# Global attention with exchanged halves by copies, merged sums and a new prologue; biases of the sparse projections added by VectorE

## The reference, cut to what matters

```
Q, K, V = x @ Wq.T + bq, x @ Wk.T + bk, x @ Wv.T + bv      # 16 heads of 8
q_scores = 0.5*norm(Q) + 0.3*entropy(softmax(Q)) + 0.2*var(Q, ddof=1)
```

```
def _rotate_half(x):
    x1, x2 = jnp.split(x, 2, axis=-1)
    return jnp.concatenate((-x2, x1), axis=-1)
q = q * cos + _rotate_half(q) * sin
k = k * cos + _rotate_half(k) * sin
attn = softmax(q @ k.T * SCALE)
return (attn @ v) @ Wo + bo
```

## Time and profile before

| | us |
|---|---|
| median of 3 runs | 3885.16 (3882.11 to 3892.41) |
| the profiled execution's own time | 3877.67 |
| its span | 3875.9 |
| PE busy | 3460.4 (89%) |
| DVE busy | 2522.3 (65%) |
| ACT busy | 1832.9 (47%) |
| POOL busy | 1613.7 (42%) |

### The profile page before, as it was taken

How to read it: one execution, slowest core, us unless ns; L and a number is a source line. 1 busy time by engine, 2 the same in 40 slices (tenths; PEclk the granted TensorE clock), 3 DMA queues, 4 the chain that set the end, 5 groups by cost and what they waited for, 6 DMA issues and landing times. The chain is left out here.

```text
span 3875.9 us, 61610 instructions
## 1 busy us (share of the span) xinstructions
PE 3460.4 (89%) x23550; PEld 2161.1 (56%) x23550; DVE 2522.3 (65%) x4730; ACT 1832.9 (47%) x3269; POOL 1613.7 (42%) x1100
## 2 busy tenths in 40 slices
PE   6999999999857647999669999999999999978997
PEld 4777787878756435777523333333333333336776
DVE  4565656565655456777567777677677766757776
ACT  2344444434323124999423334333433333339997
POOL 1212121111104123666225556556655666656664
PEclk9999999999988557999879999999999999989999
DMA  2000000000010001000100000000000000010000
GB/s 94 1 1 1 1 1 1 1 1 1 1 45 9 6 0 44 2 2 2 38 0 1 1 1 1 1 1 1 1 1 1 1 1 1 1 44 2 2 2 12
DMA packets 21486, 31.46 MB, mean 8 GB/s; under 512 B 8418, under 2 KB 17932, under 8 KB 19724
## 3 DMA queue, kind: packets, MB, share of 16 engines
q1 hardware_dynamic: 21196, 27.52, 2.3%
HBM read 26.46 MB, written 1.05 MB: 7 GB/s over the span
## 5 line engine op out<-in xcount | busy, mean ns | idle before, releaser
L3027 POOL TENSOR_TENSOR global_acc_pool<-global_acc_pool,global_probs 128x1024 f32<-128x1024 f32 x320 | 776.7, 2427 | 470.6 <-ACT global_probs L2980 452.6
L2980 ACT ACTIVATE global_probs<-global_ps 128x1024 f32<-128x1024 f32 x512 | 524.7, 1025 | 883.2 <-PE global_ps L2853 856.9
L3075 DVE TENSOR_REDUCE global_part<-global_ps 128x2 f32<-128x1024 f32 x512 | 624.7, 1220 | 428.9 <-PE global_ps L2835 428.7
L2853 PE MATMUL global_ps<-global_q,global_k 64*128 64x512 f32 x2048 | 522.4, 588 | 0.0
L2864 PE MATMUL global_ps<-global_probs,global_v 128*64 128x512 f32 x2048 | 495.7, 605 | 0.0
L2835 PE MATMUL global_ps<-global_khh,global_qhh 64*128 64x512 f32 x1024 | 324.9, 631 | 35.9 <-DVE global_part L3075 33.9
L994 DVE COPY_PREDICATED delta_Y<-delta_tri,delta_ps 128x512 f32<-128x512 uint32 x192 | 140.4, 731 | 290.9 <-PE delta_ps L533 290.9
L900 POOL TENSOR_TENSOR delta_gm<-C_tile,delta_g 128x1024 f32<-128x1024 f32 x16 | 30.4, 1897 | 718.9 <-PE delta_ps L453 685.3
L2851 PE MATMUL global_ps<-global_mrow,global_first 64*128 64x512 f32 x1024 | 323.6, 629 | 0.0
L2864 PEld LDWEIGHTS global_ps<-global_probs,global_v 128*64 128x64 f32 x2048 | 124.3, 136 | 282.6 <-issue 161.4
L2835 PEld LDWEIGHTS global_ps<-global_khh,global_qhh 64*128 64x128 f32 x1024 | 97.9, 188 | 323.0 <-DVE global_part L3075 259.3
(11 more groups left out here) (587 smaller groups left out, 6862.3 us busy)
## 6 DMA issues: line engine op xcount, KB each, us to landing
delta_cw<-in_conv_taps SPq DMA_DIRECT2D x4, 1024.0 KB, 11.5
local_tab<-in_rot_tables SPq DMA_DIRECT2D x2, 2048.0 KB, 12.3
local_tab<-in_rot_tables SPq DMA_DIRECT2D x2, 1536.0 KB, 7.9
localw_wqkv<-in_L_ffn_wqkv SPq DMA_DIRECT2D x2, 768.0 KB
delta_wqkvz<-in_L_attn_a_W_qkvz SPq DMA_DIRECT2D x1, 1024.0 KB, 6.5
local_tab<-in_rot_tables SPq DMA_DIRECT2D x2, 512.0 KB, 4.2
global_cos<-in_rope_cos SPq DMA_DIRECT2D x2, 512.0 KB, 10.2
global_sin<-in_rope_sin SPq DMA_DIRECT2D x2, 512.0 KB, 11.7
```

The costliest lines, as they stand in the source:

```text
L2853: mm = pe.matmul(ps[:, 2 * (at % 2) + s, :], k2[own, group_of(u) % 2, P * k:P * k + P], q[own, u % 3, :], start=False, stop=True)
L2980: act.activation(probs[:, at % RING, :], ps[:, 2 * (at % 2):2 * (at % 2) + 2, :].rearrange("p b n -> p (b n)"), ACT.Exp).then_inc(S["probs ...
L3027: ins = eng.tensor_tensor(sums[:, u % 2, :], sums[:, u % 2, :], probs[:, at % RING, :], ALU.add)
L3075: dve.tensor_reduce(part[:, u % 2, r % SLOTS, :], ps[:, 5:7, :], X_AXIS, ALU.max)\
```

## The change

1. Sparse stage: the bias matmuls go. DVE adds the biases while it copies q and v out of PSUM; ACT squares q from the copy. Transposes run one group ahead, and the exponentials of a group come right after the next group's projections.
2. Global stage: `wqr` and `wkr` go. ACT copies the halves of the projected block exchanged, with the sign (`swap_halves`: four copies of 32x512 out of PSUM into `swapped`), and DVE multiplies those by sin from on-chip memory. One projection for each block in place of two, at span 0 for q and 6 for k; both multiplications in one span, the sum in the next.
3. POOL adds `acc` into `acc_pool` (`merge_sums`), so `out_sums` has two matmuls in place of four; it stands in span 2, ahead of the last rough score. `invert_sums` is in span 3, `normalize_context` after tile 7, `out_rows` and `add_rows` in span 5.
4. Prologue: weights of q, k, v are loaded during the local stage before. Tables come in four column blocks with a semaphore each, `wo` last. q block 0 and keys 0 and 1 first, then four chunks of four rough scores with two pairs of banks in turn, with the other projections and the values between them. ACT scales `wq`, POOL adds `bo` to X.

```diff
-                            own = ps[:, banks[g % 2], P * t:P * t + P]
-                            pe.matmul(own, xnT[:, g % 2, P * t:P * t + P], wT[:, i, :], start=True, stop=False)
-                            mm = pe.matmul(own, ones[0:1, :], bias[0:1, :], start=False, stop=True)
+                            mm = pe.matmul(ps[:, banks[g % 2], P * t:P * t + P], xnT[:, g % 2, P * t:P * t + P], wT[:, i, :],
+                                           start=True, stop=True)
...
+                        dve.wait_ge(S["q_ps"], g + 1)
+                        dve.tensor_tensor(q_all[:, tiles, :], ps[:, Q_BANKS[g % 2], :].rearrange("p (t d) -> p t d", t=GROUP),
+                                          over_middle(bq, GROUP), ALU.add).then_inc(S["q_ready"], 1)
...
-                    weights = (wq, wqr)[part_no][:, 2 * p:2 * p + 2, :].rearrange("d h e -> d (h e)")
+                    weights = wq[:, 2 * p:2 * p + 2, :].rearrange("d h e -> d (h e)")
...
-                for n, sums in enumerate((acc, acc_pool)):
-                    for s, own in enumerate((UP, DOWN)):
-                        mm = pe.matmul(ps[own, 7, :], ones[:, 0:HD], sums[:, u % 2, BLK * s:BLK * s + BLK],
-                                       start=(n == 0), stop=(n == 1))
+                for s, own in enumerate((UP, DOWN)):
+                    mm = pe.matmul(ps[own, 7, :], ones[:, 0:HD], acc_pool[:, u % 2, BLK * s:BLK * s + BLK],
+                                   start=True, stop=True)
...
+                def swap_halves(key):
+                    n = rope_no[key]
+                    act.wait_ge(S["proj_ps"], n + 1)
+                    if n:
+                        act.wait_ge(S["rope_ready"], n)
+                    for a in range(4):
+                        b = a ^ 1
+                        ins = act.activation(swapped[32 * a:32 * a + 32, :], ps[32 * b:32 * b + 32, proj_bank(n), :], ACT.Copy,
+                                             scale=1.0 if a % 2 else -1.0)
+                    ins.then_inc(S["swap_ready"], 1)
...
+                def merge_sums(u):
+                    pool.wait_ge(S["sum_step"], (u + 1) * len(dve_adds))
+                    pool.wait_ge(S["odd_step"], (u + 1) * (TILES - len(dve_adds)))
+                    pool.tensor_tensor(acc_pool[:, u % 2, :], acc_pool[:, u % 2, :], acc[:, u % 2, :], ALU.add)\
+                        .then_inc(S["merged"], 1)
...
-                        if j in (5, 6) and next_keys(u):
+                        if j == 6 and next_keys(u):
                             if u:
                                 pe.wait_ge(S["y_done"], u)
-                            project(pe, next_keys(u), j - 5)
+                            project(pe, next_keys(u))
...
+                        if j == 0 and u + 2 < UNITS:
+                            swap_halves(("q", u + 2))
+                        if j == 6 and next_keys(u):
+                            swap_halves(next_keys(u))
...
+                    dve.wait_ge(S["swap_ready"], n + 1)
...
+                    dve.tensor_tensor(rot[:, 0, :], ps[:, proj_bank(n), :], cos[:, columns(key)], ALU.mult)\
+                        .then_inc(S["proj_read"], 1)
+                    dve.tensor_tensor(rot[:, 1, :], swapped[:], sin[:, columns(key)], ALU.mult)\
+                        .then_inc(S["rot_ready"], 1)
...
+                for c in range(CHUNKS):
+                    for qt in range(QT):
+                        rough_scores(pe, QT * c + qt)
+                        if qt == 1:
+                            if c + 2 < CHUNKS:
+                                project(pe, ("k", 0, c + 2))
+                            elif c + 2 == CHUNKS:
+                                project(pe, ("q", 1))
+                            values(2 * c)
+                        if qt == 3:
+                            values(2 * c + 1)
```

More of the change, by code:

```diff
@@ L2794, in grouped_attention @@
         with nc.Block() as block:
[L2795 to L2803 removed]
+            tables = [S["tables_" + n] for n in ("first", "second", "third", "fourth")]
@@ L2805, in _ @@
             @block.sync
             def _(sp):
[L2807 to L2814 removed]
+                load_global_weights(sp, C)
+                sp.dma_start(rows[:], W["pair_rows"]).then_inc(S["rows_loaded"], 16)
+                sp.dma_start(bo[:], W["L1_attn_b_bo"].partition_broadcast(P)).then_inc(S["rows_loaded"], 16)
@@ new lines, in _, with project @@
+                for b in range(QB):
+                    cols = slice(BLK * b, BLK * b + BLK)
+                    for half in (UP, DOWN):
+                        sp.dma_start(cos[half, cols], W["rope_cos"][:, cols]).then_inc(tables[b], 16)
+                        sp.dma_start(sin[half, cols], W["rope_sin"][:, cols]).then_inc(tables[b], 16)
+                sp.dma_start(wo[:], W["L1_attn_b_Wo"].rearrange("(c p) n -> p c n", p=P)).then_inc(S["wo_loaded"], 16)
+            def project(pe, key):
+                n = rope_no[key]
+                if n >= EARLY:
@@ L3365, in _ @@
                         load_local_weights(sp, C)
+            if stage in ("local", "global") and "global" in stages[i:] and "global" not in C:
+                C["global"] = global_weights(nc, ctx, C["inputs"])
+                C["global_loads"] = global_loads(W, C["global"])
             C["next"] = stages[i + 1] if i + 1 < len(stages) else None
```

280 lines of the change are left out of this document (157 added, 123 removed).

## The result

| | us |
|---|---|
| changed kernel, median of 4 runs | 3797.48 (3796.34 to 3801.95) |
| kernel before, median of 4 runs | 3884.28 |
| ratio | 0.9775, 95% interval 0.9758 to 0.9792 |
| forecast | 3753, range 3730 to 3795 |

What follows compares the result with a forecast made beforehand. PE's stream was taken to bound the global units, chains through several engines the other two places. Savings of 76.7 + 26.3 - 1.5 + 30.4 = 131.9 us off 3877.67, plus 7.5 for the median, gave 3753 us, range 3730 to 3795.

Steps and rivals of the forecast that it cites:

- Key units, -2.68 each: Global stage, 12 whole units with keys: two projections and the sums' saving, less a new wait and DVE load, save 2.68 us each.
- I take 0.85: the projection comes 0.5 late: Key units: place_max behind the keys' join, taken as 0.85 us against 0.36 of room, makes the next q projection 0.5 late.
- Units without keys, -2.44 each: Global stage, 17 whole units: projection 1.15, sums 0.93 and span 5's wait 0.36 save 2.44 us each.
- By the single durations it costs nothing: Global units: port contention of the sin multiplication with POOL priced at nothing; by the 2.30 to 1.22 ratio, 25 us of DVE.
- two are worth half, 0.93: Global units: with POOL's merge the sums need two matmuls, not four, saving 0.93 of 1.87 us.
- Copies 0.59, hidden: Global units: ACT's four copies a block take 0.59 us each and stay hidden, by 0.4 us on ACT.
- Rival 1: Units and prologue: copies take 1.03 each, or DVE's queue is 0.5 to 1 us late; 3772 to 3798; 17%.
- Rival 2: Global units: port contention between DVE and POOL alone costs 12 to 25 us, giving 3765 to 3778; 6%.
- Rival 3: Global units: a late merge_sums holds up PE, 31 us for each us beyond 3.3 of cover; slower than before; 4%.
- Prologue, -26.3: Global stage's prologue: a chain of three 5.3 us blocks, then DVE as bound, turns the maximum earlier; 26.3 us saved.
- End of the stage, +1.5: End of the global stage: POOL's merge of 2.43 in the open chain, less half the sums' 1.87, costs 1.5 us.
- Sparse stage, -30.4: Sparse stage: PE's group falls to 8.7 us with 8 places of 0.72; 30.4 us saved, ends 22 and 36.

Runs made afterwards that it cites:

- e1: Changed kernel with place_max put ahead of the join of the keys in span 7: 3770.0 us, ratio 0.9694.
- e10: e5 with tile 15 added by POOL, so that DVE adds four tiles of 16: 3724.94 us, ratio 0.9589.
- e5: e1 with the join of q in span 4 in place of 1 and its rounding by ACT in span 5 in place of 3: 3755.0 us, ratio 0.9665.
- e3: Changed kernel with POOL's merge taken out and the sums four matmuls again: 3800.8 us, ratio 0.9776.
- e9: e5 with POOL's merge undone, so four matmuls of sums: 3768.5 us, ratio 0.9694.
- e11: e5 with the merge behind POOL's add of tile 2 in place of tile 1: 3748.6 us, ratio 0.9643.
- e7: Changed kernel with one copy of 128x512 in place of four of 32x512, exchange and sign left out of the result: 3778.3 us, ratio 0.9717.
- e2: Changed kernel with the multiplication by sin reading the projection in PSUM, exchange left out of the result: 3775.4 us, ratio 0.9707.
- e12: Kernel before the change with tile 15 added by POOL, so that DVE adds four tiles: 3886.46 us, ratio 0.9997.

## Why the prediction was wrong

- **Key units, -2.68 each: failed, and decides the miss.** The step was "I take 0.85: the projection comes 0.5 late". The wait was seen and priced too low. The join took 1.71, and the multiplication by sin ahead of it, which wasn't counted into this wait, 2.08; the prediction's own sign came, PE waiting for `global_mrow` by 1.7 in each of the 12; span 7 grew by 2.36, and some of it ran on into spans 0 and 1 of the next unit. 12 units x 3.57 = 43 us. e1 gives 27 back with one exchange of two lines. The slowed operation was priced by a ratio (2.30 to 1.22, so 0.68 becomes up to 1.3), and that is the wrong form: DVE waits for the rest of POOL's instruction, which doesn't shrink with DVE's own size. The row used for the ratio has it too: the add of 2.30 is 1.22 left of POOL's add plus 1.08.
- **Units without keys, -2.44 each: undersized by 1.02 in 13 units, 2.1 in the three behind key units; 20 us.** The projection and span 5 came as computed. Two steps failed. "By the single durations it costs nothing": the multiplication alone did cost nothing here (0.72), but the prediction put no wait for part maxima in these spans, and the tile 15 add behind two multiplications made PE wait in span 1 (e10), the join (1.93) in span 2 (e5). And "two are worth half, 0.93": of this 0.23 was left (e3), since the merge moved POOL's row onto DVE's first add (e9, e11).
- **Copies 0.59, hidden: right as written** (588 ns, no wait for exponentials), but e7 shows that they matter through the moment of POOL's instructions. Rival 1 named the right place, DVE's queue in spans 0, 6 and 7, and a time of 3772 to 3798 that holds the result; it had 17%. Rival 2 named the right mechanism at 6% and 12 to 25 us; e2 showed 23. They are one case, not two, and its chance had been split.
- **Rival 3, the merge late for PE: fell.** PE never waited for it.
- **Prologue, -26.3: right, undersized by 5.3.** The chain of three blocks came at 5.2 each; with a first projection of 1.10 in place of 2.08 it ended 1.7 us earlier, and the 16 reductions with the three blocks among them took 24.2 (1890.19 to 1914.40) where 27.3 were reckoned.
- **End of the stage, +1.5: right** (+1.8).
- **Sparse stage, -30.4: right mechanism, undersized by 10.7**, the outer end of its own range (36) and beyond. PE's places weren't 0.72 but 0.24, in part by the clock (0.42 before at full clock), and DVE's 6.2 (6.45 computed) was the bound. The error was to take the slow duration, without a reason, for a stream that the edit itself thins.
- **The range.** The errors up (+63) and down (-16) partly cancelled. For a term of 77 us that rested on DVE keeping up in 240 spans, 3795 was too near.

## What to carry to other kernels

When work goes from the engine that is the bound to one that is 70% busy, go through its queue span by span and ask of each instruction what shares a port with it at that moment; the busy share says nothing of it. An instruction whose result another engine awaits goes ahead of one that nobody awaits yet. And after such a change the old division of work is no longer the best: the add that was free before (e12) cost 30 us after (e10).

## What the runs showed of the hardware

- A DVE instruction with both inputs in on-chip memory that starts while a POOL instruction runs ends a fixed time after it, whatever is left of it. For multiplications and joins of 128x512 (0.68 alone) that is 0.54 to 0.56 (the changed kernel, units 2 to 29: 38 of 39 multiplications, one with 0.06 left took 0.68; all 40 joins), for adds of 128x1024 (1.22 alone) 1.08 to 1.09. So the same multiplication took 0.72, 1.39, 2.08 and up to 2.88. It holds behind POOL's adds and behind its copy, and in the kernel before too.
- With one input in PSUM the multiplication takes 0.68 always (40 of 40 in e2).
- DVE's plain copy of 128x1024 takes 0.68 with POOL idle (29 of 29 in e3) and 1.25 to 2.03, 1.74 in the mean, behind its adds, ending 0.55 after them (the changed kernel).
- The other way round POOL's add, started behind an add of DVE, takes up to 3.35 in place of 2.37.
- PE's granted clock was 0.50 (1.2 GHz) from 1310 to 1330 in the kernel before, with PE busy for 19 of 20 us, and 0.92 to 1.0 in the same work of the changed kernel from 1317 to 1330. In the 10 us ahead PE had been busy for 2.2 of 10 there and, at 0.50, for 3.3 of 7 here. It wasn't chance: all 12 traces with the new sparse stage have clock 1.00 from 14 to 24 us after the stage's start, and both with the old one (the kernel before and e12) 0.50. What made the difference is open; no run was made for it.
